# Second product of the routed experts: two full-precision products of 88 rows become five products of rounded parts of 128 and 48 rows

## The reference, cut to what matters

```python
# x: (4, 512, 256); 2048 tokens, D = 256
x = x + attention0(layernorm(x)) + top-32-of-512 expression ffn(layernorm(x))
xn = layernorm(x)
x = x + L1_attn(xn) + L1_ffn(xn)
# L1_ffn: E = 16 experts, K = 2, I = 176
topk_w, topk_idx = top_k(softmax(xn @ gate_w.T), 2)
gu = einsum('th,ehj->etj', xn, w_gate_up)          # (16, 256, 352)
h  = silu(gu[..., :176]) * gu[..., 176:]
y  = einsum('eti,eih,te->th', h, w_down, combine)  # w_down (16, 176, 256)
y += swiglu(xn @ shared_gate_up) @ shared_down
```

## Time and profile before

| | |
|---|---|
| median of 3 runs (lowest, highest) | 506.53 us (505.81, 506.99) |
| profiled execution, first to last instruction (the time that it has) | 506.1 us |
| granted TensorE clock, mean | 0.997 |
| PE busy / DVE / ACT / POOL | 489.5 / 342.6 / 297.2 / 275.6 us |
| last `mw,m_ht` product | at 479 us |

### The profile page before, as it was taken

The page is one execution under the profiler, slowest core; times in us unless marked ns, Lnnn a source line. Parts: engine busy times, 40 slices in busy tenths (PEclk is TensorE's granted clock), DMA queues, the critical chain, the costliest instruction groups (busy, mean ns, idle before and its releaser), DMA issues.

```text
span 506.1 us, 7336 instructions
## 1 busy us (share of the span) xinstructions
PE 489.5 (97%) x2418; PEld 374.1 (74%) x2418; DVE 342.6 (68%) x732; ACT 297.2 (59%) x590; POOL 275.6 (54%) x253
## 2 busy tenths in 40 slices
PE   7999999989999999999999999999998999999997
PEld 5455557767887678879888888877766767677785
DVE  6999999898989999558989996224232322322347
ACT  5897898978899678589456343354331342323220
POOL 0163758749474566473634466847765665555500
PEclk9999999899999999999999999999999999999999
DMA  8900003004532011044105675722244222222177
GB/s 305 331 2 0 0 2 124 2 0 159 175 126 87 2 42 43 1 133 155 59 2 180 204 233 184 253 84 77 84 135 144 75 82 76 73 73 80 67 283 236
DMA packets 20245, 55.35 MB, mean 109 GB/s; under 512 B 3361, under 2 KB 6097, under 8 KB 20209
## 3 DMA queue, kind: packets, MB, share of 16 engines
...
...
HBM read 37.18 MB, written 17.74 MB: 109 GB/s over the span
## 4 chain that ended last, share of the span: by engine, by line
PE 71%; ACT 7%; POOL 6%; DMA 5%; issue 5%; DVE 4%; another core or an unknown queue 1%; SPq 0%; DVEq 0%; ACTq 0%
PE bank L317 50%; PE bank L510 9%; DMA y_rows<-m_y,dest 5%; PE bank L411 3%; POOL y_rows L1508 2%; POOL xg L1496 2%; PE bank L499 1%; PE bank L543 1%; PE bank L384 1%; ACT L643 1%; PE bank L570 1%; DVE m_y L1356 1%; PE bank L458 1%; ACT fd L729 1%; PE bank L400 1%
## 5 line engine op out<-in xcount | busy, mean ns | idle before, releaser
L1508 POOL DMA_INDIRECT y_rows<-m_y,dest x47 | 47.5, 1010 | 38.9 <-DVE m_y L1356 30.4
L1356 DVE TENSOR_SCALAR m_y<-bank,gslot 128x256 f32<-128x256 f32 x47 | 22.3, 483 | 61.1 <-DMA y_rows<-m_y,dest 36.6
L317 PE MATMUL bank<-mw,m_xt 128*128 x188 | 61.5, 463 | 0.8 <-DVE hs L1233 0.6
L1496 POOL DMA_INDIRECT xg<-xn_rows,tab x47 | 45.6, 971 | 20.2 <-issue 10.5
L317 PE MATMUL bank<-yhr,wsg_h 128*128 128x512 f32 x128 | 52.8, 412 | 0.0
L317 PE MATMUL bank<-hyr,wsg_h 128*128 128x512 f32 x128 | 50.0, 391 | 0.0
L317 PE MATMUL bank<-yhr,wsg_l 128*128 128x512 f32 x128 | 49.9, 390 | 0.0
L317 PE MATMUL bank<-mw,m_ht 88*128 x188 | 46.2, 381 | 3.1 <-DVE m_y L1356 2.0
L317 PEld LDWEIGHTS bank<-mw,m_xt 128*128 128x128 f32 x188 | 33.6, 189 | 17.8 <-issue 4.5
L1437 POOL TENSOR_TENSOR tk<-tk 128x512 f32<-128x512 f32 x16 | 21.0, 1315 | 38.0 <-ACT tk L787 37.9
L317 PEld LDWEIGHTS bank<-mw,m_ht 88*128 88x128 f32 x188 | 33.8, 190 | 8.7 <-issue 4.0
...
## 6 DMA issues: line engine op xcount, KB each, us to landing
...
```

The costliest lines, as they stand in the source:

```text
L317: mm = e.matmul(o, a, b, start=n == 0, stop=n == len(terms) - 1)
L1356: e.tensor_scalar(m_y[j % 3][:, :], ps("jd", j)[:, 0:D], gslot[:, j:j + 1], None, ALU.mult).then_inc(s["jy"], 1)
L1496: e.indirect_dma_start(out=xg[j % GATHERED][:, :], out_offset=None, in_=xn_d, in_offset=bass.IndirectOffsetOnAxis(ap=tab[:, j:j + 1], axis ...
L1508: e.indirect_dma_start(out=y_d, out_offset=bass.IndirectOffsetOnAxis(ap=dest[:, j:j + 1], axis=0), in_=m_y[j % 3][:, :], in_offset=None).t ...
```

## The change

Each expert's second weights are stored as 128 + 48 rows. A rounded copy and its rest are made on the chip (`mround` on ACT, `mlow` on DVE), h is split likewise after the transpose (`jhcopy`, new `jhlow`), and `xdown` is five fp32r products: rounded h by rounded w, by the rest of w, rest of h by rounded w (128 rows each), and for the last 48 rows one of 112 rows (rows 0 to 47 rounded w, rows 64 to 111 rest of w, against h doubled by a second small `jtimes` product) and one of 48. An expert takes 1472 words of `mw` and not 1216, its second load is 256 KB and not 176 KB, and the raw rows pass through scratch space: four places for experts 0 to 6, two for 7 to 15. So `experts(n)` waits for `mlow` of an earlier expert, `experts(0)` already for the stores of block 2, and `experts(7)` for rt at 22. Buffers of the tiles move into the space of the shared expert's weights `sgu`, `sdn` (new waits `past` and on dw). `vec` becomes part of `cst`. All five lists are new.

```diff
-EW = 2 * 352 + 2 * D
+UW, DW = 2 * 352, 3 * D
+EW = UW + DW
...
+        m_ht = [[tile(f"m_ht{n}{z}", D, F32R) for z in "hl"] for n in range(3)]
...
+        EARLIER = 7
+        for n in range(E):
+            lo = n * EW + UW + D
+            step = (EARLIER * EW + n % 4 * D if n < EARLIER else E * EW + n % 2 * D) - lo
+            raws.append(also(f"raw{n}", lo, 2 * step)[:, :].rearrange("p (z n) -> p z n", n=step)[:, :, 0:D])
...
+        def low_of(n):
+            return s["wus"], 4 + n + 1
...
             def hturn(j, n):
-                o = take(("jt", j), n, s["jtc"], j + 1)
+                o = take(("jt", j), n, s["x1"], 2 * NB + j + 1)
+                q.wait_ge(s["tmp"], 4)
                 q.wait_ge(s["jh"], j + 1)
-                for c in range(2):
-                    mm = e.transpose(o[0:88, c * P:(c + 1) * P], m_h[j % 3][:, c * 88:(c + 1) * 88], ident)
-                mm.then_inc(s["jt"], 1)
+                e.transpose(o[:, 0:P], m_h[j % 3][:, 0:P], ident)
+                e.transpose(o[:, P:2 * P], m_h[j % 3][:, P:2 * P], ident).then_inc(s["jt"], 1)
             def xdown(j, n):
                 o = take(("jd", j), n, s["jy"], j + 1)
-                q.wait_ge(s["jtc"], j + 1)
+                if j == 0:
+                    q.wait_ge(*low_of(E - 1))
+                q.wait_ge(s["x1"], 2 * NB + j + 1)
                 r = place[j]
-                products(o[:, 0:D], [(m_ht[j % 3][:, c * P:(c + 1) * P], mw[0:88, bass.DynSlice(r + (704 + c * D), D)]) for c in range(2)]).then_inc(s["jd"], 1)
+                w, wl, wb = (mw_r[:, bass.DynSlice(r + (UW + k * D), D)] for k in range(3))
+                h, l = m_ht[j % 3]
+                terms = [(h[:, 0:P], w), (h[:, 0:P], wl), (l[:, 0:P], w), (h[0:112, P:2 * P], wb[0:112, :]), (l[0:48, P:2 * P], wb[0:48, :])]
+                products(o[:, 0:D], terms).then_inc(s["jd"], 1)
...
+            def mround(n):
+                q.wait_ge(d_mw[n % 2], 16 * STAGED.count(n % 2) + 32 * (n // 2 + 1))
+                o = n * EW + UW
+                hi = mw_r[:, o:o + 4 * D].rearrange("p (z n) -> p z n", n=2 * D)[:, :, 0:D]
+                e.activation(hi, raws[n], ACT.Copy).then_inc(s["ph"], 1)
...
             def jtimes(j):
                 q.wait_ge(s["js"], j + 1)
-                e.tensor_tensor(m_h[j % 3][:, :], m_h[j % 3][:, :], ps("ju", j)[:, 176:352], ALU.mult).then_inc(s["jh"], 1)
+                if j > 2:
+                    q.wait_ge(s["jt"], j - 2)
+                e.tensor_tensor(m_h[j % 3][:, 192:240], m_s[j % 3][:, 128:176], ps("ju", j)[:, 304:352], ALU.mult)
+                e.tensor_tensor(m_h[j % 3][:, 0:176], m_s[j % 3][:, :], ps("ju", j)[:, 176:352], ALU.mult).then_inc(s["jh"], 1)
+            def jhlow(j):
+                q.wait_ge(s["jtc"], j + 1)
+                h, l = m_ht[j % 3]
+                e.tensor_tensor(l[:, :], ps("jt", j)[:, 0:D], h[:, :].bitcast(F32), ALU.subtract).then_inc(s["x1"], 1)
+            def mlow(n):
+                q.wait_ge(s["ph"], len(PREP) + n + 1)
+                o = n * EW + UW
+                raw = raws[n]
+                b = mw_r[64:112, o + 2 * D:o + 3 * D]
+                e.tensor_tensor(mw_r[:, o + D:o + 2 * D], raw[:, 0, :], mw_r[:, o:o + D].bitcast(F32), ALU.subtract)
+                e.tensor_tensor(b, raw[64:112, 1, :], b.bitcast(F32), ALU.subtract).then_inc(low_of(n)[0], 1)
...
             def experts(n):
...
-                    if (n + 1) * EW > fronts_at + (b - 2) * 7168:
+                    if max(n + 1, EARLIER) * EW > fronts_at + (b - 2) * 7168:
...
+                if (n + 1) * EW > front_end:
+                    q.wait_ge(s["rtm"], 8)
+                if n == EARLIER:
+                    q.wait_ge(*low_of(n - 1))
+                    q.wait_ge(s["rt"], 22)
+                elif n > EARLIER + 1:
+                    q.wait_ge(*low_of(n - 2))
+                elif 3 < n < EARLIER:
+                    q.wait_ge(*low_of(n - 4))
...
-                e.dma_start(mw[0:88, o + 704:o + EW], dn[n]).then_inc(d_mw[n % 2], 16)
+                e.dma_start(raws[n], dn[n].rearrange("p (z n) -> p z n", z=2)).then_inc(d_mw[n % 2], 16)
```

The new lists, where they matter. PE from `routed(7)` to the first tiles, and the end:

```diff
+            ...; routed(7); dgate(2, 6, 3); dgate(2, 7, 1); dup(2, 7, 2); ddown(2, 4, 6, 7); ddown(2, 5, 6, 7); dup(2, 8, 5)
+            dup(2, 9, 4); dgate(2, 8, 3); dgate(2, 9, 1); dgate(2, 10, 0); ddown(2, 6, 6, 7); ddown(2, 7, 6, 7); dgate(3, 0, 2); dgate(3, 1, 3); dup(2, 10, 5)
+            ddown(2, 8, 6, 7); ddown(2, 9, 6, 7); dup(3, 0, 1); dup(3, 1, 4); dup(3, 2, 0); ddown(2, 10, 6, 7); xturn(0, 5); xturn(1, 2); dgate(3, 2, 1)
+            dgate(3, 3, 3); ddown(3, 0, 6, 7); ddown(3, 1, 6, 7); xturn(2, 4); xturn(3, 1); dup(3, 3, 0); dgate(3, 4, 5); xturn(4, 2); xturn(5, 4)
+            ddown(3, 2, 6, 7); xup(0, 3); xup(1, 0); xup(2, 5); xup(3, 1); xup(4, 2); xturn(6, 3); hturn(0, 4); ...
```

ACT and DVE in the same stretch:

```diff
+            (ACT) mround(6); dact(2, 2); ... dact(2, 6); dact(2, 7); mround(7); dround(2, 6); mround(8); dround(2, 7)
+            mround(9); dact(2, 8); dact(2, 9); dround(2, 8); dround(2, 9); dact(2, 10); dact(3, 0); dround(2, 10); mround(10); mround(11); yround(3, 0)
+            yround(3, 1); dact(3, 1); dround(3, 0); dround(3, 1); mround(12); mround(13); dact(3, 2); dround(3, 2); jxcopy(0); jxcopy(1); jxcopy(2); dact(3, 3)
+            mround(14); mround(15); ...
+            (DVE) refine(3); dtimes(2, 5); table(); mlow(5); mlow(6); dtanh(2, 6); dtanh(2, 7)
+            dtimes(2, 6); dtimes(2, 7); mlow(7); mlow(8); mlow(9); dtanh(2, 8); dtimes(2, 8); dtanh(2, 9); dtimes(2, 9); dtanh(2, 10); dtimes(2, 10); dtimes(3, 0)
+            mlow(10); mlow(11); dout(2, 0); dout(2, 1); dtimes(3, 1); dlow(3, 0); dlow(3, 1); mlow(12); mlow(13); dtimes(3, 2); dtimes(3, 3); dlow(3, 2); jpad()
+            mlow(14); mlow(15); jtimes(0); ...
```

SP from the first experts, and POOL's `breathe`, now before the gathers (0 to 15) and behind the scatters (17 to 22):

```diff
+            (SP) yspill(2); experts(0); experts(1); experts(3); experts(2); experts(4); xstore(3); xspill(3); experts(5); park(0)
+            rback(2); yback(2); experts(6); xback(3); yspill(3); experts(7); experts(8); experts(9); experts(11); yback(3); experts(10); experts(12); experts(13)
+            park(1); experts(15); experts(14); unpark(0); ...
+            (POOL) ...; dlow(2, 5); breathe(0); ...; xfetch(1); ...; xfetch(15); yput(1); xfetch(18); yput(0); yput(2); xfetch(17); xfetch(20); yput(3); yput(5); ...
```

More of the change, by code:

```diff
@@ L194, in build @@
         g_i, g_f = tile("g_i", 32, U32), tile("g_f", 8)
-        m_xt.append(also("m_xt2", at[0], D))
-        m_ht.append(also("m_ht2", at[0] + D, D, parts=88))
+        xg[3:3] = [also(f"xg{n}", at[0] + (n - 3) * D, D) for n in range(3, 5)]
         hot, gval = tile("hot", 512), tile("gval", 32)
@@ L616, in tensor @@
-            hturn(10, 2); xdown(6, 1); xdown(7, 5); xdown(8, 3); dgate(3, 2, 4); xup(12, 2); xup(13, 1); hturn(11, 3); xturn(15, 2); xturn(16, 5)
-            xup(14, 0); xup(15, 2); xdown(9, 1); xdown(10, 4); hturn(12, 3); hturn(13, 0); dup(3, 2, 5); hturn(14, 2); hturn(15, 0); xdown(11, 4)
-            xturn(17, 1); xturn(18, 5); xdown(12, 3); xdown(13, 4); ddown(3, 1, 6, 7); xdown(14, 3); xturn(19, 0); xturn(20, 5); xup(16, 1)
-            xup(17, 2); xup(18, 0); dgate(3, 3, 4); dgate(3, 4, 1); dup(3, 3, 3); xdown(15, 0); hturn(16, 2); xup(19, 5); xturn(21, 2); xturn(22, 0)
@@ L628, in tensor @@
-            xdown(33, 0); xup(39, 3); xup(40, 1); xdown(34, 5); xdown(35, 2); xdown(36, 0); xturn(42, 5); xturn(43, 4); xup(41, 2); hturn(37, 4)
-            hturn(38, 5); dgate(3, 5, 3); xup(42, 2); xup(43, 1); hturn(39, 5); xturn(44, 0); xdown(37, 4); xdown(38, 5); hturn(40, 2); hturn(41, 0)
-            xdown(39, 4); ddown(3, 4, 6, 7); xturn(45, 0); xturn(46, 5); xdown(40, 4); xdown(41, 2); hturn(42, 3); xup(44, 4); xup(45, 1)
-            xup(46, 5); hturn(43, 4); hturn(44, 1); hturn(45, 0); xdown(42, 3); xdown(43, 5); xdown(44, 1); hturn(46, 3); dup(3, 5, 0); xdown(45, 3)
@@ L634, in tensor @@
+            xturn(45, 3); xturn(46, 1); xdown(41, 4); xdown(42, 5); xup(45, 3); xup(46, 2); hturn(44, 1); xdown(43, 4); hturn(45, 0); hturn(46, 5); xdown(44, 3)
+            xdown(45, 2); xdown(46, 1); dup(3, 5, 4); dup(3, 6, 0); dup(3, 7, 3); dgate(3, 6, 5); dgate(3, 7, 2); dgate(3, 8, 1); ddown(3, 5, 6, 7)
+            ddown(3, 6, 6, 7); dgate(3, 9, 4); dgate(3, 10, 5); ddown(3, 7, 6, 7); dup(3, 8, 0); dup(3, 9, 2); dup(3, 10, 1); ddown(3, 8, 6, 7); ddown(3, 9, 6, 7)
             ddown(3, 10, 6, 7)
@@ L1529, in sync @@
+            breathe(21); breathe(22)
         @block.sync
```

416 lines of the change are left out of this document (222 added, 194 removed).

## The result

The kernel after takes 538.4 us (median of 4 runs, 534.3 to 543.8), where the kernel before took 506.8 us in the same session (505.8 to 508.3): a ratio of 1.0545, 95% interval [1.0501, 1.0588]. (Two of the four executions, over 542 us, were disturbed and are left out of the ratio.) It is slower, and by more than my slower rival said: the prediction was 497.3 us, with 490 to 504 as its range. The profiled execution took 534.3 us, with a span of 532.5. Part of it belongs to that session, as the last experiments show: in a later session, on another chip, the unchanged kernel after took 526.3 us, ratio 1.0407 [1.0337, 1.0477]. It is slower all the same.

A forecast was written before the change was run, and what follows sets the result against it. The prediction took PE to bound the kernel, busy for 489.5 of 506.1 us. From 506.1 it took 12.2 (products) and 0.6 (start), added 3 (late loads), 1 (earlier waits) and 0 (end): 497.3 us, range 490 to 504.

The forecast's parts named there:

- my slower rival: Experts' loads before the tiles run one expert at a time: 24.4 us of stall, 517.7 us in all; chance 0.11.
- PE's work: In the tile stage, five products of xdown take 0.60 us in place of 0.86, saving 12.2 us over 47 tiles.
- PE's waits before 240: At the start, vec in cst saves 0.6 us; early mround waits on ACT and SP add part of 1 us.
- waits behind 320: loads, tiles, end: Late experts' loads stall PE 3 us; the tiles keep their 5.9 us of PE idling and the end adds 0.
- my 0.60: Time of xdown per tile in us: five fp32r products at 0.12 each, narrow ones at full price.
- My bounds: For xdown's five products: 0.12 us each at the low end, 0.215 each (1.08 in all, losing 10.3 us) at the high.
- rival (5): Register work between xdown's products keeps them at 0.16 us, giving back 9.4 us: 506.7 us, no change; chance 0.05.
- my 0 to 8: Bounds in us of PE's stall for the late experts' loads before xup(0), taken as 3.
- my 352: Time in us when the nine late experts' loads are done, at 8.2 for two and 37 for nine.
- rival (4): Same as my slower rival: loads take 56 us for nine experts; decides once the last expert lands after 360; chance 0.11.
- rival 2: POOL becomes the bound of the tile stage; 6 us of waits for scatters reach PE: 503.3 us; chance 0.12.
- The signs I had asked for: Right: PE busy near 477 us, xdown at 0.60, xup(0) near 349. Wrong, for products: starts 0.15 us or more apart.

The follow-up runs named there:

- e16: The kernel after, unchanged, run again in a later session on another chip: 526.3 us, ratio 1.0407 to the kernel before.
- e2: Also written e2_l112: the kernel after with the fifth product of xdown on 112 rows in place of 48; 511.7 us, ratio 1.0108 to the kernel before.
- e6: e2 with mlow of experts 0 to 6 cut to one memset, leaving out their low parts; 505.0 us, ratio 0.9976 to the kernel before.
- e1: The kernel after with the fifth product of xdown on 48, 64, 80, 96, 112 or 128 rows by turns; 519.9 us (one run).
- e3: The kernel before with the new orders up to routed(7), the old ones behind, and no rounding of experts' weights; 526.4 us, ratio 1.0429.
- e4: The kernel after with own scratch places for experts 7 to 13, whose loads no longer wait for mlow; 526.3 us, ratio 1.0372 to the kernel before.
- e8: The kernel before with vec in the columns of cst and no load of its own; 507.6 us (one run).

## Why the prediction was wrong

The sum of the prediction, term by term, against the first profile of the kernel after and against e16, span 523.1, which has none of the waits without a releaser:

| term | predicted | after (532.5) | e16 (523.1) |
|---|---|---|---|
| PE's work | -12.2 | +8.1 | +7.0 |
| PE's waits before 240 | -0.6, and part of +1 | +5.8 | +6.6 |
| 240 to 320 | the rest of +1 | +4.3 | +4.3 |
| waits behind 320: loads, tiles, end | +3, 0, 0 | +8.2 | -0.9 |
| sum | -8.8 | +26.4 | +17.0 |

**Products: the step that failed.** "I give those of 112 and 48 rows the full price, since no row says that fewer rows are cheaper." No row said either that 48 rows were not dearer, and 0.12 came from products on the full 128. The one product of 48 rows costs 0.34 to 0.38 us more than its 0.12, so `xdown` went from 0.86 to 0.98 in place of 0.60. Over 47 tiles that is 17.1 us, of the 19.2 by which PE's work is off in e16 (+7.0 in place of -12.2); one more stretch of low clock there is an estimated 1.7. With 112 rows (e2, e6) my 0.60 held. My bounds reached to 1.08, so the true value lay within them, but my range was built round the lower one. I had put the upper bound's chance into rival (5) at 0.05 and at 0.16 us a product, and with a wrong cause: register work costs nothing (e1). The kernel before has 88 rows here, and e1 puts the step between 64 and 80.

**The orders: not priced at all.** I took for granted that "the new lists" were at least even before 240 us. They cost 6.4 us at `oproj(3, 0)` and, without the new work, at `routed(7)` (e3). `oproj(3, 0)` came by 220.9 in every profile with the old front and not before 224.8 in any with the new one, so this is no scatter. Which wait to blame was not tested.

**DVE from 240 to 320: seen, and hidden too easily.** I counted five `mlow` ahead of `table` in a stretch where "DVE is 93% full", put `tab` 3.5 us later and wrote "PE doesn't wait for it directly". `tab` was written 12 us later (320.2 against 308.1). PE does wait, for `dtanh` and `dtimes` behind them in DVE's list: 4.3 us, and 4.8 come back at `routed(7)` when `mlow` is left out (e6 against the kernel after). At 93% there was no cover.

**Loads: size right, the worth of a wait wrong.** `xup(0)` at 365.7, not 349, but 317.1 + 40.6 = 357.7 was the earliest by my own sum of PE's work; PE stood still for 6.8 us on the way, within my 0 to 8, and 4.0 in e16 against the 3 I took. Nine loads took 40.5 us, 324.1 to 364.6 (37 forecast). The load of expert 7 came 7.0 us behind the end of `routed(7)`, where I had 9. There is luck in the stall: the loads landed 12.6 us after my 352, and it came out right because PE was 11 us late too. The waits for `mlow` are worth little: nothing within the chain (e4), since the landing of the load two before takes their place. The last load did land after the 360 at which rival (4) was to decide, but because the first went out at 324 and not 315; one expert at a time, 56 us for nine, did not happen.

**Tiles and POOL: right.** POOL did not bound (rival 2). In e16 PE is idle for 0 us between `xup(0)` and the last `xdown`, where it was 6.5 before. DVE's wait for the scatters in the whole span fell from 36.6 us to 13.1 in e2_l112 and to 2.2 in e16, so longer tiles explain only a part of it (waits of the profile of e16: total, times, longest):

```profile
DVE m_y L1420 <- DMA y_rows<-m_y,dest: 2.2, 2, 1.2
```

**Start.** It stays open. The kernel after started 0.8 us later, not 0.6 earlier, but the landing of this load scatters by 2 us over the profiles (e8), so neither sign is shown, and I should have had a range from more than one row.

The signs I had asked for told it at once: PE's work was not near 477, and starts stood more than 0.15 us apart, though at the narrow product alone and not between all.
